# Unused rows of the stacked keys: SBUF-to-SBUF copies by DMA replaced by memsets on GpSimd

## The reference, cut to what matters

```python
x = L0_attn_x
x = _layernorm(x + _L0_attn_ref(x, ...), axis=-1)   # y = y * silu(gate); y @ W_out; residual + y
x = _layernorm(x + _L0_ffn_ref(x, ...), axis=-1)    # softmax router, argmax, gate * (x @ expert_w[idx] + b)
x = _layernorm(x + _L1_attn_ref(x, w_Q, w_K, w_V), axis=-1)
#   scores = einsum('bhtd,bhsd->bhts', q, k) / sqrt(HD); probs = softmax(scores); attn = probs @ v
x = _layernorm(x + _L1_ffn_ref(x, ...), axis=-1)    # six nodes of multi-head attention
```

## Time and profile before

| | us |
|---|---|
| median of three runs | 2202.36 |
| profiled execution | 2200.61 |
| its span | 2198.8 |
| TensorE busy | 2025.9 (92%) |
| VectorE busy | 1728.6 (79%) |
| ScalarE busy | 1489.5 (68%) |
| GpSimd busy | 314.4 (14%) |
| chain of waits, TensorE | 81% |
| chain of waits, VectorE | 13% |
| chain of waits, DMA | 0% |

### The profile page before, as it was taken

How to read it: one execution, slowest core, us unless ns; L and a number is a source line. 1 busy time by engine, 2 the same in 40 slices (tenths; PEclk the granted TensorE clock), 3 DMA queues, 4 the chain that set the end, 5 groups by cost and what they waited for, 6 DMA issues and landing times.

```text
span 2198.8 us, 32024 instructions
## 1 busy us (share of the span) xinstructions
PE 2025.9 (92%) x10812; PEld 841.4 (38%) x10812; DVE 1728.6 (79%) x3501; ACT 1489.5 (68%) x2004; POOL 314.4 (14%) x370
## 2 busy tenths in 40 slices
PE   5748987999999999999999999999999999999995
PEld 2224443333333333444444444444444444443331
DVE  6846887788888878777787788777777888778884
ACT  4743552666666677777777777777777777776664
POOL 1100211000000011111111111111111111113213
PEclk9977885999999999999999999999999999999998
DMA  3001234233333366566666656656555565655530
GB/s 104 19 24 58 82 89 103 45 74 73 74 73 73 83 113 114 110 109 110 110 109 109 109 104 108 108 105 112 102 110 107 108 109 109 109 108 100 95 58 25
DMA packets 137899, 200.25 MB, mean 91 GB/s; under 512 B 20290, under 2 KB 55770, under 8 KB 137178
## 3 DMA queue, kind: packets, MB, share of 16 engines
q1 hardware_dynamic: 137742, 198.25, 46.5%
HBM read 75.45 MB, written 23.73 MB: 45 GB/s over the span
## 4 chain that ended last, share of the span: by engine, by line
PE 81%; DVE 13%; issue 4%; ACT 2%; POOL 0%; DMA 0%; DVEq 0%; POOLq 0%; SPq 0%; ACTq 0%
PE bank_s L1044 27%; PE bank_o L1082 22%; PE bank_x L1067 7%; DVE nm L1399 5%; PE bank_m L1095 3%; PE bank_x L1030 3%; PE bank_x L1009 3%; PE bank_x L1017 2%; PE bank_m L1115 2%; PE bank_x L996 2%; PE bank_x L1141 2%; PE bank_s L947 1%; PE bank_m L1105 1%; PE bank_m L1054 1%; DVE big L1288 1%
## 5 line engine op out<-in xcount | busy, mean ns | idle before, releaser
L1399 DVE TENSOR_REDUCE nm<-bank_s 128x1 f32<-128x512 f32 x2048 | 1334.9, 684 | 341.0 <-PE bank_s L1044 339.9
L834 ACT ACTIVATE big<-bank_x 128x1024 f32<-128x1024 f32 x1024 | 1049.8, 1026 | 482.5 <-PE bank_x L1067 455.8
L1044 PE MATMUL bank_s<-kst,qst 62*128 62x512 f32 x2048 | 836.9, 469 | 48.3 <-DVE nm L1399 47.6
L1067 PE MATMUL bank_x<-qst,kst 64*128 64x512 f32 x2048 | 749.3, 447 | 1.6 <-ACT big L834 1.6
L1044 PEld LDWEIGHTS bank_s<-kst,qst 62*128 62x128 f32 x2048 | 358.6, 187 | 687.2 <-DVE nm L1399 598.4
L1082 PE MATMUL bank_o<-big,at 128*32 128x512 f32 x4096 | 554.4, 614 | 2.2 <-ACT big L834 2.0
L1067 PEld LDWEIGHTS bank_x<-qst,kst 64*128 64x128 f32 x2048 | 303.9, 186 | 10.2 <-issue 6.0
L618 POOL CAST at<-at 128x512 fp32r<-128x512 f32 x112 | 68.2, 609 | 1272.9 <-ACT at L765 1036.2
L620 POOL TENSOR_TENSOR at<-at 128x512 fp32r<-128x512 f32 x112 | 143.2, 1278 | 10.0
L1082 PEld LDWEIGHTS bank_o<-big,at 128*32 128x32 f32 x4096 | 81.1, 108 | 153.0 <-issue 149.1
L842 ACT ACTIVATE big<-bank_x,big 128x128 f32<-128x128 f32 x256 | 69.2, 379 | 27.9 <-DVE big L1436 15.8
(11 more groups left out here) (154 smaller groups left out, 1470.3 us busy)
## 6 DMA issues: line engine op xcount, KB each, us to landing
at<-nodes_d SPq DMA_DIRECT2D x144, 256.0 KB, 5.8
kst<-at SPq DMA_DIRECT2D x288, 128.0 KB
qst<-at SPq DMA_DIRECT2D x288, 128.0 KB
nodes_d<-big SPq DMA_DIRECT2D x48, 256.0 KB, 3.0
at<-w_d SPq DMA_DIRECT2D x48, 193.0 KB, 5.9
at<-x2T_d SPq DMA_DIRECT2D x32, 256.0 KB, 4.6
kst<-at SPq DMA_DIRECT2D x128, 64.0 KB
qst<-at SPq DMA_DIRECT2D x128, 64.0 KB
```

Source lines behind the costliest of these rows:

```text
L834: act.activation(PT[:, kp, h, :, :], ring.take()[0].rearrange("p (c n) -> p c n", c=2), ACT.Exp, scale=x.c.scale).then_inc(S["c_ex"], 1)
L1044: pe.matmul(bank_s[:, n % 2, :], qst[rows, x.r, h, t * P:(t + 1) * P], kst[rows, x.r, h, :], start=True, stop=True).then_inc(S["c_s_ps"], 1)
L1067: mm = pe.matmul(sec(to, j), kst[rows, x.r, h, kc_ * P:(kc_ + 1) * P], qst[rows, x.r, h, :], start=True, stop=True)
L1399: dve.tensor_reduce(nm[:, k, at_n:at_n + 1], bank_s[:, n % 2, :], AX.X, ALU.max, negate=True).then_inc(S["c_red"], 1)
```

## The change

The DMA copies are gone, and the semaphore `c_fill` with them. GpSimd runs the five memsets in turns 2, 4, 6 and 8, for the slots 0 to 3, each when y of batch 2r + 1 is done. It no longer waits for `b_xT_ev`. `stack` of unit u < 4 waits until 5u + 5 memsets are done.

```diff
-                    sp.wait_ge(S["c_fill"], 16 * 3 * min(x.u + 1, RING - 1))
+                    sp.wait_ge(S["c_ones"], 5 * x.u + 5)
...
-            def fill(r):
-
-                sp.wait_ge(S["b_y"], 2 * r + 3)
-                sp.wait_ge(S["c_ones"], 5)
-                if r > 1:
-                    sp.wait_ge(S["c_fill"], 16 * 3 * (r - 1))
-                sp.dma_start(kst[:, r, :, :].bitcast(F32), kst[:, r - 1, :, :].bitcast(F32)).then_inc(S["c_fill"], 16)
-                for f in range(2):
-                    empty = slice(f * HALF + kc.R, f * HALF + kc.RS)
-                    sp.dma_start(qst[empty, r, :, :].bitcast(F32), qst[empty, r - 1, :, :].bitcast(F32)).then_inc(S["c_fill"], 16)
-
...
-                if b in (5, 7, 9):
-                    fill(b // 2 - 1)
...
-                if b == 2:
-                    pool.wait_ge(S["b_y"], 3)
-                    pool.wait_ge(S["b_xT_ev"], b + 2)
-                    pool.memset(kst[:, 0, :, :].bitcast(F32), 1.0).then_inc(S["c_ones"], 1)
-                    pool.wait_ge(S["c_ones"], 1)
+                if b in (2, 4, 6, 8):
+                    r = b // 2 - 1
+                    pool.wait_ge(S["b_y"], 2 * r + 3)
+                    pool.memset(kst[:, r, :, :].bitcast(F32), 1.0).then_inc(S["c_ones"], 1)
+                    pool.wait_ge(S["c_ones"], 5 * r + 1)
                     for f in range(2):
                         first = f * HALF + kc.R
                         for t in (kst, qst):
-                            pool.memset(t[first:first + kc.RS - kc.R, 0, :, :].bitcast(F32), 0.0).then_inc(S["c_ones"], 1)
-                    pool.wait_ge(S["c_ones"], 5)
+                            pool.memset(t[first:first + kc.RS - kc.R, r, :, :].bitcast(F32), 0.0).then_inc(S["c_ones"], 1)
+                    pool.wait_ge(S["c_ones"], 5 * r + 5)
```

More of the change, by code:

```diff
@@ L235, in build @@
               "stk3", "m_dma", "s_ps", "red", "nm_ok", "st_ps", "ex", "pv_ps", "store", "link", "pool", "sum", "xlink", "plink",
-              "x2in", "x3", "x3out", "mv", "rs", "ones", "fill")
+              "x2in", "x3", "x3out", "mv", "rs", "ones")
         class Kind:
```

## The result

The changed kernel takes 2220.16 us (median of four runs, 2218.78 to 2220.67) where the kernel before took 2204.06 us (median of four, 2200.61 to 2206.40) in the same comparison: a ratio of 1.0072, 95% interval 1.0057 to 1.0086. It is slower by about 16 us, with the interval from 12.6 to 19 us. It was right in its sign and in the wide range. The step that it forecast was 25.7 us where the runs show 16, and two of its three terms were wrong in size.

A forecast was written before the change was run, and what follows sets the result against it. Bound taken: the second stage's chain of waits round VectorE, TensorE and ScalarE. 17.6 + 6.1 + 2 = 25.7 us on the profiled 2200.61 us gave 2226; own range 2221 to 2235, with rivals 2205 to 2235.

The forecast's parts named there:

- (a): Turns 2, 4, 6: VectorE's four normalise pieces alternate with GpSimd's memsets, ending behind memset five; 6.0 + 6.0 + 5.6 = 17.6 us.
- Rival B: Turns 2, 4, 6: all four normalise pieces run behind memset two; 1.2 us a turn, 2210 us in all; chance 0.15.
- rival C: Memsets don't block VectorE; only GpSimd's queue in turn 8 costs, 5.6 us, giving 2206 us; chance 0.16.
- (b): Turn 8: GpSimd's split queues behind the burst, so ScalarE's copy, which overwrites the split's buffer, starts 6.1 us late.
- (c): TensorE's granted clock stays low longer after the stops: 2 us in all, bounds 0 and 2.1 us at each.
- Removed copies: Nine SBUF-to-SBUF DMAs off SyncE in turns 5, 7, 9: taken as 0, with 2.4 us kept for the range.

The follow-up runs named there:

- e4: Changed kernel without the two memsets of kst to zero, so three memsets in each burst: 2217.36 us, ratio 1.0056.
- e7: Kernel before, DMA fills kept, its one burst in turn 2 no longer waiting for ScalarE's copy: 2204.90 us, ratio 1.0013.
- e11: Changed kernel with every memset cut into four of 512 elements a partition, same bytes: 2207.55 us, ratio 1.0019.
- e2: Changed kernel with the burst of slot 3 moved from turn 8 to turn 9, behind the split: 2217.81 us, ratio 1.0057.
- e1: Changed kernel with the wait for ScalarE's copy put back ahead of the bursts of turns 2, 4 and 6: 2208.65 us, ratio 1.0026.
- e6: Changed kernel with three extra TensorE products, output never read, at the end of turns 2, 4 and 6: 2213.79 us, ratio 1.0048.
- e3: Changed kernel with bursts of turns 2, 4, 6 waiting for ScalarE's copy again and slot 3's burst in turn 9: 2204.14 us, ratio 1.0010.
- e10: Kernel before with extra TensorE products, output never read, among the 36 scores ahead of the attention loop: 2207.95 us, ratio 1.0018.
- e9: Kernel before with the extra products of e10 and one more product at the end of turns 1 to 5: 2207.55 us, ratio 1.0018.

## Why the prediction came out as it did

**(a), 17.6 us for turns 2, 4 and 6: the mechanism right, the size wrong.** Measured is 3.43 - 1.12 = 2.31 us a turn, 6.9 in all; less the 0.3 us that ScalarE's copy hides in turn 6 (TensorE started 0.38 us behind the normalise there before, 0.06 in the changed kernel), 6.6 on the path. The step that failed is "the third memset asked before the second piece did, so it goes first": piece two had started at 222.43, 1.07 us before the third memset, and it passed together with piece one. The row I had leaned on the earlier trace rows showed GpSimd between pieces three and four, where piece four was not yet waiting. It was a case of order of arrival, and I read a strict taking of turns from it. Rival B (one gap, 1.2 us) was wrong the other way; the truth lay between, nearer to B: B stops the normalise for one memset, the runs show two, and I had four. That a memset blocks (against rival C) stands in the rows above and in e4, e7 and e11.

The Trainium skill, "SBUF — State Buffer", section "Who interferes with whom", says that a VectorE operation in a two-port mode contends with GpSimd, whoever issues first keeping the ports for its whole instruction, and that the order of issue decides who blocks. The trace agrees with both in turn 2: a memset blocks, the piece ends 0.08 us behind it, and piece two, issued before memset three, goes before it. In e11 the first piece lost to a memset that started 0.16 us later.

**(b), 6.1 us for turn 8: right.** Measured 5.85, with the releaser named (GpSimd's L607 ahead of ScalarE's L755), gone from the tail in e2, kept in e1. The burst and split took 358.92 - 347.53 = 11.4 us against 11.5 in the sum. That VectorE's late normalise lay under this wait was right, and e4 brought it to light; its size was not, since it is 1.6 us late (2.71 against 1.10) and not 5.2, by the same error as in (a).

**(c), 2 us for the clock: too small.** Turns 2 to 7 lost 13.1 us, of which 6.6 are the blocks. The 6.5 that remain I put down to the clock, within the bounds of 0 to 8.4 given for four places: the time at 1.2 GHz rose from 37.6 to 51.2 us, and e6, which brings it to 34.1, returns 6.8 us with the blocks in place. It is a difference and not a sum of measured products. The step that failed is "part of each slow stretch is there already": it is, but a stop of 3.6 us in TensorE lengthened it into the critical products of the next turn (L1134 and L1154 at 2.00 and 1.80 us, against 1.05 and 0.99 behind a normalise that stands alone). The taken value was an argument from plausibility where the bounds were wide.

**Removed copies, 0: right.** e3 has neither copies nor exposed memsets and repeats the turns of before to 0.06 us. The 0.8 us that I kept in the range was not the copies: e3's turn 4 has none beside it and takes 20.13 us, its turn 3 19.27, with 6.8 and 3.4 us at the low clock, as in the kernel before.

**The sum.** 17.6 + 6.1 + 2 = 25.7 was forecast; 6.6 + 5.9 + 6.5 = 19.0 was measured in the profile and 16 us in the medians, whose interval (12.6 to 19 us) just reaches the stage's account. That the total came within 6 us of the result is in part luck: (a) was 11 us too high and (c) 4.5 too low. With (a) right and (c) as forecast the sum would have been 14.7 us, or 2215, below the forecast's own range.

## What to carry to other kernels

An instruction that is free on an idle engine can block another engine's: look at what runs beside it at the moment when it will be issued, and count how many of its pieces are waiting, not only that one is. A filler job belongs behind the moment when the critical short operation has passed, and long memsets cut into short ones took most of the stop away in e11, though nothing of the queue behind the burst. A stop on a path that feeds TensorE can cost twice: its own length, and the clock in the work behind it, from 0.9 us for the one of e7 to 6.5 for the changed kernel's three.

## What the runs showed that I had not expected

- Between two back-to-back memsets, two waiting pieces of 128x128 pass, and three of 128x64. The memset behind them is stretched by 0.11 to 0.14 us (1.94 and 1.91 against 1.80 us).
- A TENSOR_SCALAR of 128x4 is held up as a large one is (1.27 us for its usual 0.17), and so is a CAST of 128x16, while RECIPROCAL (0.17), reductions (1.90) and TENSOR_TENSOR kept their time beside memsets of the old burst, as L1440 did in the earlier trace rows.
- Three products whose output is never read, 2.74 us of TensorE, made the changed kernel's turns 2 to 7 shorter by 6.8 us; the like among the scores (e10, e9) made the kernel before slower by 0.18%.
- Cutting 20 long memsets into 80 short ones of the same bytes moved turns 2 to 7 from 13.1 to 1.7 us over before.
